# Attention's side products made in a free score bank instead of the bank of turned probabilities

## The reference

```
xn  = layernorm(x)
Q   = (xn @ Wq).reshape(n, s, 4, 4, 64)      # 4 groups, 4 heads in each
K,V = (xn @ Wk), (xn @ Wv)                   # 4 groups of 64
raw = einsum('bsgwe,btge->bstgw', Q, K / 8)
A   = einsum('bstgw,btge->bsgwe', softmax(raw, over t), V)
s   = xn + A @ Wpost
```

## Time and profile before

| | busy us | share of the span |
|---|---|---|
| TensorE matmul (PE) | 2350.0 | 83% |
| TensorE weight load (PEld, beside PE) | 1333.7 | 47% |
| VectorE (DVE) | 1961.2 | 69% |
| ScalarE (ACT) | 1815.4 | 64% |
| GpSimd (POOL) | 1738.2 | 61% |

### The profile page before, as it was taken

One profiled execution on the slowest core, in us unless ns is written; L12 is line 12 of the kernel. 1 busy time (PEld: TensorE's weight loads), 2 busy tenths in 40 slices (PEclk: granted clock), 3 DMA queues, 4 the chain that ended last, 5 costly groups with the idle time before them and its releaser, 6 DMA issues.

```text
span 2844.3 us, 37619 instructions
## 1 busy us (share of the span) xinstructions
PE 2350.0 (83%) x12740; PEld 1333.7 (47%) x12744; DVE 1961.2 (69%) x2958; ACT 1815.4 (64%) x3324; POOL 1738.2 (61%) x1416
## 2 busy tenths in 40 slices
PE   5776889998688989898988898989898888887771
PEld 4443567775334454445444454445444544452331
DVE  5778745543347776676677666776677677779898
ACT  3557834346277776777676766786677567766752
POOL 1000165416747896878587768876976598745565
PEclk9888899999799999999999998999998999998895
DMA  5000169865535676555564465447543654466776
GB/s 154 19 19 5 56 187 255 227 183 86 93 94 118 117 153 136 118 107 128 134 122 92 100 157 109 95 91 172 106 91 79 163 109 91 95 155 144 177 158 150
DMA packets 282048, 344.44 MB, mean 121 GB/s; under 512 B 66175, under 2 KB 211534, under 8 KB 281856
## 3 DMA queue, kind: packets, MB, share of 16 engines
q0 software_dynamic: 84080, 175.67, 33.6%
q1 hardware_dynamic: 175264, 144.80, 17.5%
q10 hardware_dynamic: 22512, 21.57, 2.2%
HBM read 198.23 MB, written 26.80 MB: 79 GB/s over the span
## 4 chain that ended last, share of the span: by engine, by line
PE 32%; ACT 16%; DVE 9%; issue 9%; POOL 7%; DMA 1%; DVEq 0%; POOLq 0%; ACTq 0%
PE bank L1935 5%; PE bank L1964 4%; PE bank L1798 4%; PE bank L1746 4%; DVE bank L1546 4%; PE bank L1787 3%; ACT PT L1012 3%; POOL arena L1671 3%; PE bank L1857 2%; ACT Pr L1021 2%; ACT bank L1154 2%; POOL acc_sb L1649 2%; PE bank L1810 2%; PE bank L2000 1%; PE bank L2032 1%
## 5 line engine op out<-in xcount | busy, mean ns | idle before, releaser
L1671 POOL TENSOR_TENSOR arena<-arena 128x512 f32<-128x512 f32 x512 | 862.1, 1760 | 32.5 <-DVE arena L1537 32.0
L1246 DVE TENSOR_REDUCE negmax<-bank 128x1 f32<-128x512 f32 x512 | 342.2, 680 | 268.7 <-PE bank L1787 268.2
L1649 POOL DMA_INDIRECT acc_sb<-ybuf,slot_idx x256 | 422.3, 1650 | 146.7 <-DMA ybuf<-arena 64.3
L1154 ACT ACTIVATE bank<-arena,A_sb 128x512 f32<-128x512 f32 x512 | 353.6, 694 | 195.3 <-DVE arena L1551 170.0
L1677 POOL TENSOR_TENSOR arena<-arena 128x512 f32<-128x512 f32 x192 | 285.6, 1488 | 311.9 <-DVE arena L1546 311.8
L1021 ACT ACTIVATE Pr<-bank,negmax 128x512 f32<-128x512 f32 x512 | 358.1, 699 | 116.6 <-DVE negmax L1246 116.3
L1798 PE MATMUL bank<-ident,Pr 128*128 128x128 f32 x2048 | 339.3, 290 | 109.9 <-ACT PT L1012 86.2
L1546 DVE TENSOR_TENSOR_SCAN bank<-bank,arena 128x512 f32<-128x512 f32 x320 | 390.6, 1221 | 49.3 <-ACT bank L1154 40.7
L1012 ACT COPY PT<-bank 128x512 f32<-128x512 f32 x512 | 301.8, 590 | 146.6 <-PE bank L1798 128.5
L1787 PE MATMUL bank<-Kp,Qp 64*128 64x512 f32 x1024 | 314.1, 692 | 75.5 <-ACT Pr L1021 59.9
L1798 PEld LDWEIGHTS bank<-ident,Pr 128*128 128x128 f32 x2048 | 229.3, 145 | 293.8 <-issue 157.7
(11 more groups left out here) (218 smaller groups left out, 3905.3 us busy)
## 6 DMA issues: line engine op xcount, KB each, us to landing
arena<-arena POOLq DMA_DIRECT2D x255, 512.0 KB, 5.1
arena<-bc_dram SPq DMA_DIRECT2D x256, 256.0 KB, 3.8
ybuf<-arena ACTq DMA_DIRECT2D x64, 256.0 KB
arena<-in_w_gate SPq DMA_DIRECT2D x64, 128.0 KB, 3.1
arena<-in_w_up SPq DMA_DIRECT2D x64, 128.0 KB, 3.6
arena<-in_w_down SPq DMA_DIRECT2D x64, 128.0 KB, 4.6
arena<-in_X SPq DMA_DIRECT2D x8, 512.0 KB, 9.0
s_sb<-in_X SPq DMA_DIRECT2D x8, 512.0 KB, 6.0
```

Source lines behind the costliest of these rows:

```text
L1154: act.activation(bank[DECAY[g % 2]][:, :], dt_sb[:, size_slot(b, cb), :], ACT.Exp, scale=A_sb[:, cb, n:n + 1]).then_inc(ssm_decay, 1)
L1246: dve.tensor_reduce(negmax[:, m % RING_STAT:m % RING_STAT + 1], bank[m % RING_S_ATT][:, :], AX.X, ALU.max, negate=True).then_inc(att_max, 1)
L1649: pool.indirect_dma_start(acc_sb[:, i, :], None, ybuf, bass.IndirectOffsetOnAxis(ap=slot_idx[:, b * TILES + i, k:k + 1], axis=0), bounds_c ...
L1671: pool.tensor_tensor(st_sb[:, g % RING_S, :], u_sb[:, size_slot(b, cb), :], B_sb[:, load % RING_BC, :], ALU.mult).then_inc(ssm_input, 1)
```

## The change

The three side products leave bank 3. `spare(n) = (n + 1) % 3` names the score bank that is free at an odd step n: step n-2's scores have been exponentiated, and the next scores have not been made. The products now come at odd steps: keys at step 1, the spread at 3, queries at 5 of a pair, behind the turn of that step and ahead of `values`, which is no longer cut in halves. Each product waits for the exponential of step n-2. The scores that follow wait for the product's copy, since they use its bank. `turn_p` waits no more for any of these copies. On ScalarE the copy of the product stands between the copy of the turned tile and the exponential of the same step, where before it stood behind the exponential.

```diff
+K_AT, SPREAD_AT, Q_AT = 1, 3, 5
-    PROJ = PROBT
+    def spare(n):
+        return (n + 1) % RING_S_ATT
 # ScalarE, att_step, behind act.copy(PT...) and ahead of the exponential
+                p, at = n // PAIR_STEPS, n % PAIR_STEPS
+                if at == K_AT and p + 1 < PAIRS and p % 2:
+                    self.copy_k(b, (p + 1) // 2, spare(n))
+                if at == SPREAD_AT and p >= 1:
+                    w.wait_ge(att_invmm, PAIRS * b + p)
+                    w.wait_ge(att_at, PAIRS * b + p - 1)
+                    act.copy(inv_bc[:, :], bank[spare(n)][:, :]).then_inc(att_invbc, 1)
+                if at == Q_AT and p + 1 < PAIRS:
+                    self.copy_q(b, p + 1, spare(n))
...
-                if at == 2 and p >= 1:
...
-                    act.copy(inv_bc[:, :], bank[PROJ][:, :]).then_inc(att_invbc, 1)
-                if at == 4 and p + 1 < PAIRS:
-                    self.copy_q(b, p + 1, PROJ)
-                if at == 6 and p + 1 < PAIRS and p % 2:
-                    self.copy_k(b, (p + 1) // 2, PROJ)
 # TensorE
-            def product_q(self, b, p):
-                w.wait_ge(att_k, GROUPS * b + p // 2 + p % 2)
-                w.wait_ge(att_invbc, PAIRS * b + p - 1)
-                w.wait_ge(att_pt, b * ATT_STEPS + PAIR_STEPS * (p - 1) + 5 - LAG_T)
-                self.product(Wq_sb[:, :, p * P:(p + 1) * P], PROJ).then_inc(att_qmm, 1)
+            def product_q(self, b, p, n):
+                w.wait_ge(att_exp, b * ATT_STEPS + n - 1)
+                self.product(Wq_sb[:, :, p * P:(p + 1) * P], spare(n)).then_inc(att_qmm, 1)
...
 # score
+                pair, at = n // PAIR_STEPS, n % PAIR_STEPS
+                if at > K_AT and pair % 2 and pair + 1 < PAIRS:
+                    w.wait_ge(att_k, GROUPS * b + (pair + 1) // 2 + 1)
+                if at > SPREAD_AT:
+                    w.wait_ge(att_invbc, PAIRS * b + pair)
+                if at > Q_AT and pair + 1 < PAIRS:
+                    w.wait_ge(att_q, PAIRS * b + pair + 2)
 # turn_p
-                w.wait_ge(att_q, PAIRS * b + min(p + 1 + (at > 4), PAIRS))
-                w.wait_ge(att_k, GROUPS * b + min(p + (at > 6), PAIRS - 1) // 2 + 1)
-                w.wait_ge(att_invbc, PAIRS * b + (p - (at <= 2) if p else 0))
 # spread
-                w.wait_ge(att_pt, b * ATT_STEPS + min(PAIR_STEPS * (p + 1) + 3 - LAG_T, ATT_STEPS))
+                w.wait_ge(att_exp, b * ATT_STEPS + min(n - 1, ATT_STEPS))
...
 # att_step
                 if n % 2 == 0:
                     if n < ATT_STEPS:
                         self.score(b, n)
-                    if self.other(b, p, at) and 0 <= n - LAG_AV < ATT_STEPS:
-                        self.values(b, n - LAG_AV, (0, 1))
-                elif 0 <= n - 1 - LAG_AV < ATT_STEPS:
-                    self.values(b, n - 1 - LAG_AV, (2, 3) if self.has_other(p, at - 1) else (0, 1, 2, 3))
...
+                    return
+                if at == K_AT and p + 1 < PAIRS and p % 2:
+                    self.product_k(b, (p + 1) // 2, n)
+                if at == SPREAD_AT and p >= 1:
+                    self.spread(b, p - 1, n)
+                if at == Q_AT and p + 1 < PAIRS:
+                    self.product_q(b, p + 1, n)
+                if 0 <= n - 1 - LAG_AV < ATT_STEPS:
+                    self.values(b, n - 1 - LAG_AV)
```

More of the change, by code:

```diff
@@ L1027, in att_step @@
                     act.copy(rowinv[:, :, :], wide(rowrec[:, :], [[1, PAIR_STEPS], [0, HD]])).then_inc(att_inv, 1)
-                if at == 2 and p >= 1:
-                    w.wait_ge(att_invmm, PAIRS * b + p)
-                    w.wait_ge(att_at, PAIRS * b + p - 1)
-                    act.copy(inv_bc[:, :], bank[PROJ][:, :]).then_inc(att_invbc, 1)
-                if at == 4 and p + 1 < PAIRS:
-                    self.copy_q(b, p + 1, PROJ)
-                if at == 6 and p + 1 < PAIRS and p % 2:
-                    self.copy_k(b, (p + 1) // 2, PROJ)
             def exp_step(self, n):
@@ L1747, in product, with product_k @@
                 return ins
[L1749 to L1753, removed]
-            def product_q(self, b, p):
-                w.wait_ge(att_k, GROUPS * b + p // 2 + p % 2)
-                w.wait_ge(att_invbc, PAIRS * b + p - 1)
-                w.wait_ge(att_pt, b * ATT_STEPS + PAIR_STEPS * (p - 1) + 5 - LAG_T)
-                self.product(Wq_sb[:, :, p * P:(p + 1) * P], PROJ).then_inc(att_qmm, 1)
+            def product_k(self, b, g, n):
+                w.wait_ge(att_exp, b * ATT_STEPS + n - 1)
+                self.product(Wk_sb[:, :, g * P:(g + 1) * P], spare(n)).then_inc(att_kmm, 1)
+            def product_q(self, b, p, n):
+                w.wait_ge(att_exp, b * ATT_STEPS + n - 1)
+                self.product(Wq_sb[:, :, p * P:(p + 1) * P], spare(n)).then_inc(att_qmm, 1)
             def att_lead(self, b, j):
@@ L1789, in turn_p @@
             def turn_p(self, b, m):
-                p, at = (m + LAG_T) // PAIR_STEPS, (m + LAG_T) % PAIR_STEPS
                 w.wait_ge(att_exp, b * ATT_STEPS + m + 1)
@@ L1799, in turn_p, with values @@
                 ins.then_inc(att_turned, 1)
-            def values(self, b, m, chunks):
+            def values(self, b, m):
                 p, i, _ = att_place(m)
@@ L1807, in values @@
                 g = p // 2
-                for c in chunks:
+                for c in range(TILES):
                     for j in range(2):
@@ L1811, in values, with spread @@
                                         start=(c == 0), stop=(c == TILES - 1))
-                if c == TILES - 1:
-                    ins.then_inc(att_av, 1)
-            def spread(self, b, p):
+                ins.then_inc(att_av, 1)
+            def spread(self, b, p, n):
                 w.wait_ge(att_inv, PAIRS * b + p + 1)
-                w.wait_ge(att_q, PAIRS * b + min(p + 2, PAIRS))
-                w.wait_ge(att_k, GROUPS * b + min(p + 1, PAIRS - 1) // 2 + 1)
-                w.wait_ge(att_pt, b * ATT_STEPS + min(PAIR_STEPS * (p + 1) + 3 - LAG_T, ATT_STEPS))
+                w.wait_ge(att_exp, b * ATT_STEPS + min(n - 1, ATT_STEPS))
                 for i in range(TILES):
-                    ins = pe.transpose(bank[PROJ][:, i * P:(i + 1) * P], whole(rowinv[:, 2 * i:2 * i + 2, :]), ident[:, :])
+                    ins = pe.transpose(bank[spare(n)][:, i * P:(i + 1) * P], whole(rowinv[:, 2 * i:2 * i + 2, :]), ident[:, :])
                 ins.then_inc(att_invmm, 1)
```

## The result

The changed kernel took 2758.88 us (median of 4 runs, 2755.18 to 2761.86) against 2852.7 us for the kernel before (median of 4): a ratio of 0.9675, 95% interval 0.9661 to 0.9688. The sign and, in the main, the mechanism were right, the size was not.

What follows compares the result with a forecast made beforehand. TensorE and ScalarE passing bank 3 and the score banks bound the late attention. Spreads 23 us plus products 35 us, 58 us, weighed by 57% to 33, plus 1 for the front: 34 us less, 2818 us; range 2786 to 2855.

Steps and rivals of the forecast that it cites:

- What bounds the kernel: Attention beside the scan: no engine is full; TensorE and ScalarE passing bank 3 and the score banks set the pace.
- The unit price of a product, 0.58 us: Queries and keys, late batches: the stretch around one product falls from 6.36 to 5.78 us; 60 products give 35 us.
- The unit price of a spread, 0.48 us: Spreads, late batches: the stretch around one falls from 4.92 to 4.44 us; 48 spreads give 23 us.
- The weight of 57%: Share of the chain held by TensorE's and ScalarE's attention lines, used to weigh 58 us down to 33 us.
- The first two batches, 1 us: Batches at the front, 36 items: routing and experts set the pace, so 1 us gained, between 0 and 17.
- The cover of 0.20 us for the exponential: Scores behind a product: values and turn, 1.62 us on TensorE, cover copy and exponential, 1.42 us on ScalarE.
- Rival A: Attention beside the scan: a scan no faster swallows the gain, no change, 2852 us; chance 0.17, counted with another rival.
- Rival B: Scores behind a product: the exponential comes late, losing 0.49 us at each of 60 products, 2868 us; chance 0.15.
- Rival C: TensorE's clock in the six late stretches: it rises too, 27 us on top of 34, 2791 us; chance 0.16.

Runs made afterwards that it cites:

- order_only: Changed kernel's order on every engine, but the products stay in bank 3: 2923.08 us, ratio 1.0217 to the kernel before.
- dose_before: Kernel before, with the four transposes of each spread issued twice in batches 2 to 7: 2872.25 us, ratio 1.0078 to the kernel before.
- values_first: Changed kernel, but at odd steps the values stand ahead of the product, not behind it: 2833.38 us, ratio 0.9948 to the kernel before.

## Why the prediction was wrong, step by step

- *What bounds the kernel*: right for the late batches. TensorE and ScalarE passing banks to each other set the pace; `order_only` shows how much the shared bank costs.
- *The unit price of a product, 0.58 us*: too small. In the pair above it is 5.73 less 4.98 = 0.75 us, and the shortest intervals with queries in the two traces are as long (5.73 and 4.97). The after side of my sum took the product at the 1.92 us that it has behind the scores; behind a turn it takes 0.21 us less with the turn.
- *The unit price of a spread, 0.48 us*: too small as well. I reckoned both sides at TensorE's pace (3.85 us after, from scores to scores), but the pair above took 4.94 and 4.35 us, ScalarE being late. I wrote that with a decay between, ScalarE sets the pace in both kernels, and did not price it: through one bank a late ScalarE holds TensorE up at each passage, so the saving there was 0.59 us. The mean over all was 0.70.
- *The weight of 57%*: this is the step that failed most. It took a share of the chain's lines for the share of the saving that is on the path, and so made 33 us of the 58 in the six late batches. The traces have 61 us less in the intervals and 68 from the third batch's first scores to the end, and `dose_before` shows time added at the spreads nearly whole in the kernel's time (22 us of 21 to 25). With the prices of the two pairs, 60 x 0.75 + 48 x 0.59 = 73 us, and no weight, the sum comes near the 68. This was added up afterwards and is no test, and it agrees in the sum more than in the parts: an interval with queries fell by 0.49 us in the mean, less than its 0.75, and one with a spread by 0.70, more than its 0.59.
- *The first two batches, 1 us*: too small, 13 us measured. I let the routing stretch stand for both batches, but the second batch's attention lies in the experts' stage. Its busy times, which I had not set beside the others (first scores to last, 321 to 699 us, TensorE 344 of 377 us), show TensorE busy for 91% of it, nearer to a bound than in the late stretches (85% in the stretch shown above). These intervals fell from 377.3 to 363.0 us, those of the first batch from 221.5 to 216.8. But the same instructions of the second batch took 363 to 384 us in five traces, so the traces don't divide the 13 us between the two batches. The row before:

```profile
321.40:698.70 377.30, 343.66 (x2115) 246.37 (x2112) 179.80 (x357) 178.99 (x410) 173.03 (x156) 0.97 0.68 182
```

- *The cover of 0.20 us for the exponential*: right in its parts (0.10, 0.48, 0.79 in the interval shown), and right that it was enough. `values_first` shows the loss without it.
- *Rival A*, absorbed: wrong; GpSimd took the faster attention out of its waits for VectorE, 246.7 us where 311.8 stood in the trace before.
- *Rival B*, slower: didn't happen. *Rival C*, the clock: about 6 us by the estimate above, not the 27 us that it named.
- *What stays open*: of the 94 us, the late batches alone gave 55 us by the ratio of all runs and 66 to 68 by three of the four and by the trace, and the first two gave 9 to 18. That leaves some 13 to 26 us beside the 13 measured for the first two, which lie within what three comparisons and the stretch ahead of the third batch leave open (equal kernels differ by 24 us there). How the gain divides between a free bank and the new order is open too.

No run beat the changed kernel.

## What to carry to other kernels

When a wait on a shared bank is taken away, don't multiply its price by the share that the lines have of the chain of waits. Here that share was 57%, and time added at the same place came back nearly whole (22 us of 21 to 25 us). A known dose at the place of the change, put into the kernel before, tells the weight; read from the trace what the dose really adds, since here it was 0.43 us and not 0.58. Price both sides of an interval from a place where the other engine is late too, since a bank that two engines pass to and fro lets a late copy hold up the next turn. And when a copy is put ahead of work that others wait for, count what stands between on the waiting engine; that cover (the values here) carried 78 of the 94 us.

## What the runs showed of the hardware

What a group of matmuls takes depends here on what stands ahead of it. A product (two matmuls of the program, four records of 128x512) behind two scores started with its first weight load at 888.06 and reached the values 1.92 us later. Behind four transposes its first weights loaded 0.11 us ahead of it, beside the last transpose, it started 0.49 us after their start, and it took 1.81 us. The transposes, which take 0.56 to 0.59 us with values behind them, took 0.49 to the product's start. Together that is 0.21 us less for each product.

The same holds for transposes behind transposes: four took 0.56 us up to the values, eight 0.99, so the second four cost 0.43.
